# Side work of the key and value jobs reordered in a gated cross-attention kernel

## The reference

```python
h = layernorm(x)                        # x: 32 sequences of 64 tokens, 512 wide
q = rope(h @ wq)                        # 32 heads of 128
k, v = rope(ctx @ wk), ctx @ wv         # 8 key/value heads of 128
attn = softmax(q k^T / sqrt(128) + mask)
x = x + tanh(g_xattn) * ((attn v) @ wo)
h = layernorm(x)
logits = h @ route_w.T                  # 8 experts, top 1, weighted by its logit
x = x + tanh(g_ffn) * lora(h, A[e], B[e])   # rank 16
```

## Time and profile before

| | us |
|---|---|
| median of 3 runs | 1186.3 |
| lowest, highest | 1183.96, 1186.74 |
| the profiled execution: its own time | 1188.29 |
| its span, first to last instruction | 1186.3 |
| PE busy | 1128.3 (95%) |
| DVE busy | 921.5 (78%) |
| ACT busy | 632.5 (53%) |
| POOL busy | 567.9 (48%) |
| mean granted TensorE clock | 0.987 of full speed |

### The profile page before, as it was taken

How to read it: one execution, slowest core, us unless ns; L and a number is a source line. 1 busy time by engine, 2 the same in 40 slices (tenths; PEclk the granted TensorE clock), 3 DMA queues, 4 the chain that set the end, 5 groups by cost and what they waited for, 6 DMA issues and landing times.

```text
span 1186.3 us, 17218 instructions
## 1 busy us (share of the span) xinstructions
PE 1128.3 (95%) x5792; PEld 925.9 (78%) x5792; DVE 921.5 (78%) x1408; ACT 632.5 (53%) x1090; POOL 567.9 (48%) x517
## 2 busy tenths in 40 slices
PE   7899899779999999999999999999999999999997
PEld 6688788667777787777777777888888888888775
DVE  7773755768787888787888888888888888778886
ACT  6352345546666665656665544555555555555441
POOL 4650457866676666666663323233333333333320
PEclk9899899889999999999999999999999999999999
DMA  6869955374444444454448825542424353522201
GB/s 226 250 194 358 302 174 221 106 276 160 160 160 160 168 167 168 168 175 169 163 147 308 302 65 169 187 167 92 161 89 160 105 193 115 167 89 98 63 1 72
DMA packets 88902, 197.89 MB, mean 167 GB/s; under 512 B 8304, under 2 KB 41200, under 8 KB 82928
## 3 DMA queue, kind: packets, MB, share of 16 engines
q1 hardware_dynamic: 88816, 196.79, 48.6%
HBM read 113.92 MB, written 82.84 MB: 166 GB/s over the span
## 4 chain that ended last, share of the span: by engine, by line
PE 51%; POOL 14%; DVE 14%; issue 13%; ACT 4%; DMA 2%; SPq 1%; DVEq 0%; POOLq 0%; ACTq 0%
PE attn L845 18%; PE proj L783 13%; PE score L800 4%; POOL rot L1570 4%; PE attn L735 4%; PE turned L735 2%; DVE o_s L1117 2%; DVE q_r L1032 2%; POOL wq_s L1545 2%; DVE p_low L1110 2%; PE score L735 2%; PE turned L811 2%; DVE acc L1129 2%; PE attn L827 1%; ACT p_high L1391 1%
## 5 line engine op out<-in xcount | busy, mean ns | idle before, releaser
L845 PE MATMUL attn<-wo_s,o_s 128*128 128x512 f32 x1536 | 384.5, 399 | 15.9 <-DVE o_s L1117 15.9
L783 PE MATMUL proj<-xB,wq_s 128*128 128x512 f32 x1344 | 345.1, 400 | 7.8 <-DVE q_r L1074 5.1
L845 PEld LDWEIGHTS attn<-wo_s,o_s 128*128 128x128 f32 x1536 | 280.6, 188 | 87.2 <-DVE o_s L1117 31.4
L1570 POOL TENSOR_TENSOR rot<-rot,tab 128x512 f32<-128x512 f32 x160 | 216.8, 1356 | 224.5 <-ACT rot L1354 224.4
L783 PEld LDWEIGHTS proj<-xB,wq_s 128*128 128x128 f32 x1344 | 249.5, 190 | 69.1 <-DVE q_r L1074 5.9
L1037 DVE TENSOR_TENSOR q_r<-q_r,rot 128x512 f32<-128x512 f32 x128 | 124.8, 975 | 47.5 <-POOL rot L1570 36.6
L1399 ACT ACTIVATE o_s<-attn 128x512 fp32r<-128x512 f32 x128 | 69.6, 596 | 148.3 <-PE attn L831 148.1
L1032 DVE TENSOR_TENSOR q_r<-q_r,tab 128x512 f32<-128x512 f32 x128 | 140.7, 1099 | 3.1 <-ACT rot L1354 3.0
L1129 DVE SCALAR_TENSOR_TENSOR acc<-attn,gates_t,acc 128x512 f32<-128x512 f32 x128 | 96.0, 750 | 52.9 <-PE attn L845 50.9
L800 PEld LDWEIGHTS score<-k_r,q_r 128*128 128x128 f32 x1024 | 124.3, 192 | 7.3 <-issue 2.6
L800 PE MATMUL score<-k_r,q_r 128*128 128x64 f32 x1024 | 121.8, 272 | 0.2 <-DVE prob_even L1094 0.2
(11 more groups left out here) (174 smaller groups left out, 1485.2 us busy)
## 6 DMA issues: line engine op xcount, KB each, us to landing
wq_kept<-wq_s SPq DMA_DIRECT2D x16, 1792.0 KB, 6.6
wq_s<-wq_kept SPq DMA_DIRECT2D x16, 1792.0 KB, 8.7
v_kept<-vst SPq DMA_DIRECT2D x64, 256.0 KB, 4.1
v_s<-v_kept SPq DMA_DIRECT2D x128, 128.0 KB, 4.9
wo_kept<-wo_s SPq DMA_DIRECT2D x32, 512.0 KB, 2.9
wo_s<-wo_kept SPq DMA_DIRECT2D x32, 512.0 KB, 5.8
k_kept<-kst SPq DMA_DIRECT2D x32, 256.0 KB, 2.2
wq_raw<-in_wq SPq DMA_DIRECT2D x16, 512.0 KB, 7.7
```

What stands on the lines that cost most here:

```text
L783: last = e.matmul(dst[:, :], wq_s[:, b % 2, A, s, kt, :], xB[:, B, mv, kt, :], start=(first and kt == 0 and m == 0), stop=(kt == 1 and m = ...
L845: last = e.matmul(attn[bp][:, :], o_s[:, s, bp, h, :], wo_s[n % WO_SLOTS][:, m, :], start=(h == 0 and i == 0), stop=(h == GROUP - 1 and i ...
L1570: e.tensor_tensor(r3, r3, sin, ALU.mult).then_inc(times_sin, 1)
```

## The change

- `VST` goes from 3 to 4: four staging places for values.
- `X_BESIDE` moves each pair one or two jobs earlier (9, 12, 14, 17, 34, 37, 40, 43 become 8, 11, 13, 16, 32, 35, 38, 41), `X_TURN` goes from 3 to 4, and `combine_x` stands at the head of GpSimd's next job. The first pair of x is fetched one job earlier.
- The low halves of wv(2,1), wv(3,1), wo0, wo1 and wo2 move from GpSimd to VectorE. From job 56 on VectorE makes a weight's low half in the job itself and behind its `rope_add`.
- The store and the later fetch of each `xB` block have a semaphore of their own, so ScalarE waits for the blocks it overwrites next, not for all seven.
- On GpSimd the ropes' `by_sin` stand ahead of `combine_weights` and `weight_low` in each job. In step 0 the first rope and the low halves of (3, 0) and (3, 1) stand ahead of `combine_weights(3)`.
- VectorE masks the first scores ahead of finishing job 62, GpSimd subtracts their maximum at the head of job 62, and ScalarE takes the exponential at its end rather than behind job 63.
- ScalarE splits the pieces (3, 2) and (3, 3) in step 1 and no longer at the end of step 0.

```diff
-VST, KST = 3, 4
+VST, KST = 4, 4
...
-X_BESIDE = {9: 4, 12: 5, 14: 6, 17: 7, 34: 0, 37: 1, 40: 2, 43: 3}
-X_TURN, X_PLACES = 3, 3
+X_BESIDE = {8: 4, 11: 5, 13: 6, 16: 7, 32: 0, 35: 1, 38: 2, 41: 3}
+X_COMBINE, X_TURN, X_PLACES = 1, 4, 3
...
-X_FETCH = [7, 8, 9] + [n + X_TURN + 1 for n in list(X_BESIDE)[:-X_PLACES]]
+X_FETCH = [6, 8, 9] + [n + X_TURN + 1 for n in list(X_BESIDE)[:-X_PLACES]]
...
 def low_on_vector(w):
-    return w[0] in ("ctx", "wk") or (w[0] == "wo" and w[1] % GROUP == 3)
+    if w[0] == "wo":
+        return w[1] < GROUP or w[1] % GROUP == 3
+    return w[0] in ("ctx", "wk") or (w[0] == "wv" and w[2] == 1 and w[1] >= 2)
...
@@ vector, jobs
+                if n == SCORES_AFTER:
+                    mask_scores(0)
                 finish_job(n)
...
-                for w in SPLITS_BESIDE.get(n + 1, ()):
+                for w in SPLITS_BESIDE.get(n + 1, ()) if n + 1 < KEYS_3_MADE else ():
                     raw_low(w)
                 finish_key(JOBS[n])
+                for w in SPLITS_BESIDE.get(n, ()) if n >= KEYS_3_MADE else ():
+                    raw_low(w)
...
-                if n == SCORES_AFTER:
-                    mask_scores(0)
@@ scalar
-                    elif X_NO[pair] == CHUNK_TILES and i == 0:
-                        e.wait_ge(xB_stored, 16 * BLOCKS)
+                    elif X_NO[pair] == CHUNK_TILES:
+                        for B in range(BLOCKS)[2 * i:2 * i + 2]:
+                            e.wait_ge(xB_moved[B], 16)
...
+                if n == SCORES_AFTER:
+                    exponential(0)
...
-            exponential(0)
...
-                if k % 2 == 0:
+                if k % 2 == 0 or k == 1:
                     for w in weights_of(k):
                         wq_split(*w)
...
-                if k % 2 == 0:
+                if k % 2 == 0 and k:
                     for w in weights_of(k + 1):
                         wq_split(*w)
@@ gpsimd, jobs
-                for w in SPLITS_BESIDE.get(n, ()):
+                early = n < VALUES_MADE
+                if n == SCORES_AFTER:
+                    subtract_max(0)
+                for w in SPLITS_BESIDE.get(n, ()) if early else ():
                     raw_low(w)
+                if n - X_COMBINE in X_BESIDE:
+                    combine_x(X_BESIDE[n - X_COMBINE])
                 if n in X_BESIDE:
                     x_norms(X_BESIDE[n])
+                if JOBS[n][0] == "k":
+                    by_sin(ROPE_NO[JOBS[n]])
+                if n in ROPE_BESIDE:
+                    by_sin(ROPE_NO["q", *ROPE_BESIDE[n]])
                 if n in COMBINED_BESIDE:
                     combine_weights(COMBINED_BESIDE[n])
                 for w in WQ_BESIDE.get(n, ()):
                     weight_low(*w)
-                if JOBS[n][0] == "k":
-                    by_sin(ROPE_NO[JOBS[n]])
-                if n in ROPE_BESIDE:
-                    by_sin(ROPE_NO["q", *ROPE_BESIDE[n]])
-                if n in X_BESIDE:
-                    combine_x(X_BESIDE[n])
-                if n == SCORES_AFTER:
-                    subtract_max(0)
+                for w in SPLITS_BESIDE.get(n, ()) if not early else ():
+                    raw_low(w)
@@ gpsimd, step 0
+                    for q in ropes[0]:
+                        by_sin(ROPE_NO["q", *q])
+                    weight_low(*pieces[0])
+                    weight_low(*pieces[1])
+                    for q in ropes[1]:
+                        by_sin(ROPE_NO["q", *q])
+                    combine_weights(pieces[0][0])
+                    for q in ropes[2]:
+                        by_sin(ROPE_NO["q", *q])
```

More of the change, by code:

```diff
@@ L346, in build @@
         first_in = [sem(f"first_in{i}") for i in range(len(FIRST))]
-        xB_in = [sem(f"xB_in{i}") for i in range(BLOCKS)]
+        xB_moved = [sem(f"xB_moved{i}") for i in range(BLOCKS)]
         raw_in = [sem(f"raw_in{i}") for i in range(RAW)]
@@ L357, in build @@
         wo_stored = [sem(f"wo_stored{i}") for i in range(WO_SLOTS)]
-        xB_stored = sem("xB_stored")
         stored = [sem(f"stored{t}") for t in range(HALF_TILES)]
@@ L597, in store_xB @@
                 e.dma_start(xB_kept[B].rearrange("p h k n -> p (h k n)"),
-                            xB[:, B].rearrange("p h k n -> p (h k n)").bitcast(F32)).then_inc(xB_stored, 16)
+                            xB[:, B].rearrange("p h k n -> p (h k n)").bitcast(F32)).then_inc(xB_moved[B], 16)
             def fetch_xB(i):
@@ L602, in fetch_xB @@
                 e.wait_ge(produced, BLOCKS * (HEAD_PAIRS_ALL - 1) + i + 1)
-                if i == 0:
-                    e.wait_ge(xB_stored, 16 * BLOCKS)
+                e.wait_ge(xB_moved[B], 16)
                 e.dma_start(xB[:, B].rearrange("p h k n -> p (h k n)").bitcast(F32),
-                            xB_kept[B].rearrange("p h k n -> p (h k n)")).then_inc(xB_in[B], 16)
+                            xB_kept[B].rearrange("p h k n -> p (h k n)")).then_inc(xB_moved[B], 16)
             for w in FIRST[:BEFORE_JOBS]:
@@ L773, in product @@
                 if b == HEAD_PAIRS_ALL:
-                    e.wait_ge(xB_in[B], 16)
+                    e.wait_ge(xB_moved[B], 32)
                 if b < HEAD_PAIRS_ALL:
@@ L1610, in _ @@
                     subtract_max(k)
-                if pieces and k % 2 == 0:
-                    combine_weights(pieces[0][0])
[L1613 to L1624, removed]
+                    if pieces and k % 2 == 0:
+                        combine_weights(pieces[0][0])
+                    if pieces and k % 4 == 3:
+                        weight_low(*pieces[0])
+                    normalise(k)
+                    if pieces and k % 4 != 3:
+                        weight_low(*pieces[0])
+                    for q in ropes[0]:
+                        by_sin(ROPE_NO["q", *q])
+                    if pieces:
+                        weight_low(*pieces[1])
+                    for q in ropes[1] + ropes[2]:
+                        by_sin(ROPE_NO["q", *q])
+                else:
+                    for q in ropes[0]:
+                        by_sin(ROPE_NO["q", *q])
+                    weight_low(*pieces[0])
+                    weight_low(*pieces[1])
+                    for q in ropes[1]:
+                        by_sin(ROPE_NO["q", *q])
+                    combine_weights(pieces[0][0])
+                    for q in ropes[2]:
+                        by_sin(ROPE_NO["q", *q])
                 for n in wo_late(k):
```

## The result

The changed kernel takes 1173.15 us (median of 4 runs, 1171.59 to 1174.4) against 1185.38 us for the kernel before in the same session (1183.96 to 1186.74): a ratio of 0.9896, 95% interval 0.9878 to 0.9915, or 12.2 us less. Its profiled execution took 1174.4 us by its own time, 1172.3 of it span, against 1188.29 and 1186.3: 14.0 us less in the span. The forecast was 1170, or 16.4 us less.

A forecast was written before the change was run, and what follows sets the result against it. TensorE was taken to bound the kernel, with idle and half-clock time before 270 us to win back. Gains of 5.2 (A), 6.2 (B) and 5.0 (196 to 270 us) sum to 16.4: median 1170 us, range 1159 to 1180.

The forecast's parts named there:

- Hole A: TensorE's 4.8 us wait in job 12 for a low half of wv from GpSimd; gain 2.2 plus spell 3.0.
- The walk without turn-taking: Job 12: if VectorE and GpSimd don't alternate, wv(3,1) ends at 44.6 and the stall is 1.1 us; forecast took 2.6.
- the spell: TensorE's time at the lower clock (1.2 of 2.4 GHz) after a hole, priced at 3.0 us each.
- Hole B: TensorE's 3.2 us wait in the transposes after job 37 for GpSimd's sums of x; gain 3.2 plus spell 3.0.
- rival 4: Fourth staging place swallowed by full DMA queues and hole B stays: 1176 us, chance 0.08.
- Holes C and D: Waits ahead of product (1,3), 2.0 us for ScalarE's copy, and (1,6), 4.5 us for VectorE's sum; together give 1.0.
- Hole E: Waits of 1.1 us before first probability transposes, 4.6 before first values product; stage 196 to 270 us gives 5.0.
- the 32 us to be had: Most the change could give before 270 us: 20.2 us of holes and 12 of lower-clock spells.
- Later steps keep their order and their cost.: From 270 us to the end the span changes by no more than 2 us.
- Rival 1: GpSimd and VectorE hold each other up less; product (1,6) waits under 2 us: 1161 us, chance 0.2.
- rival 2: Stage of ropes gives nothing or job 12 keeps its spell: 1175 to 1178 us, chance 0.2.
- nor 3: Rival: moved blocks delay the rope chain on GpSimd between jobs 56 and 63: slower, 1194 us, chance 0.05.

The follow-up runs named there:

- e8: Changed kernel with three staging places for values (VST 3) as before, instead of four: 1174.15 us, ratio 0.9896.
- e2: Kernel before, with the changed kernel's order from job 48 on only: 1183.03 us, ratio 0.9967.
- e10: Changed kernel with 16 extra matmuls, whose result nobody reads, on TensorE before product (1,6): 1174.54 us, ratio 0.990.
- e4: Changed kernel run again unaltered, for a second profile: 1173.17 us (of three executions), ratio 0.9889.
- e11: Changed kernel run again unaltered, in a later session: 1174.43 us, ratio 0.9878.
- e3: Changed kernel with VectorE's query sums (1,1) and (1,2) in job 59 instead of job 60: 1173.9 us, ratio 0.9888.
- e7: Changed kernel with GpSimd's combine_weights(2) and four weight halves in its idle time, and sums (1,1), (1,2) in job 59: 1172.15 us, ratio 0.9884.
- e9: Changed kernel with GpSimd's three blocks and VectorE's low halves of wo1 and wo2 moved into idle time: 1171.8 us, ratio 0.9876.

## Why the prediction was right, and where it was not

**Hole A: 5.2 forecast, 5.1 measured, in part by luck.** The walk without turn-taking was the right one for VectorE. Its rows around the two halves of wv, and GpSimd's for the sums of x beside them:

```profile
41.71 0.69 DVE L1028 TENSOR_TENSOR ctxT<-near_raw,ctxT 128x512 fp32r<-128x512 f32 x1
42.31 0.68 DVE L1028 TENSOR_TENSOR wv_s<-near_raw,wv_s 128x512 fp32r<-128x512 f32 x1
42.92 0.68 DVE L1053 TENSOR_TENSOR vst<-turned,vst 128x512 fp32r<-128x512 f32 x1
43.52 0.68 DVE L1028 TENSOR_TENSOR ctxT<-near_raw,ctxT 128x512 fp32r<-128x512 f32 x1
44.12 0.68 DVE L1028 TENSOR_TENSOR wv_s<-near_raw,wv_s 128x512 fp32r<-128x512 f32 x1
44.72 0.68 DVE L1053 TENSOR_TENSOR vst<-attn,vst 128x512 fp32r<-128x512 f32 x1
```

```profile
41.88 1.72 POOL L1560 TENSOR_TENSOR combined<-raw 128x256 f32<-128x256 f32 x1 [0.96 <-DVE raw L1008]
43.55 1.84 POOL L1561 TENSOR_TENSOR combined<-raw 128x256 f32<-128x256 f32 x1
...
198.59 0.74 POOL L1540 TENSOR_TENSOR combined<-wq_raw 128x256 f32<-128x256 f32 x1
```

wv(3,1) was ready at 44.8 (44.12 + 0.68), and job 12 waited 0.8 us for it, not 2.6. VectorE, whose instructions followed each other without a gap, was not slowed; GpSimd's sums took 1.7 to 1.8 us, where one of the same shape took 0.74 elsewhere. They came late for their transposes, and TensorE waited 1.2 there, 2.0 in all. The two engines do hold each other up, but who pays was not known. The hole thus gave 2.8, not 2.2, and the spell 2.3, not 3.0; the two errors cancel. The Trainium skill (SBUF — State Buffer, section "Who interferes with whom") has it that the order of issue decides who blocks. These rows agree in part: each sum began just behind a half of VectorE (41.88 behind 41.71, 43.55 behind 43.52) and was held up. But the halves at 42.31 and 44.12 began after the sums and were not. Each sum ended with VectorE's next instruction that reads PSUM (42.92 + 0.68 = 43.60, and 45.4). No spell followed, as forecast.

**Hole B: 6.2 forecast, 6.3 measured.** 3.2 of hole and 3.1 for its spell. e8 shows that the fourth place, to which the prediction gave a share, has none that can be told: that half of rival 4 holds. e2 shows that the spell of before was not certain: with the hole at 2.98 us it did not come. That the profile of before had it is luck for the sum.

**Holes C and D: 1.0 forecast, 2.0 measured.** C went as said, and D stayed, on the engine and in the size said (4 to 6 us; it was 4.6, the walk had 5.9). The walk charged turns to nearly every rope_add, which was too much (of the five from 203 to 217 us two took 1.78, one 1.21 and two 0.7), and none to wo2's low half, put at 0.6, which took 1.75.

**Hole E: the stage from job 48, 5.0 forecast, 6.0 measured (17.2 - 11.2).** C and D alone give 1.0 more than forecast; behind them two errors of 0.7 cancel. The lead gained up to the values product was forecast at 3.5 and is 5.2 (16.4 - 11.2); what follows it, the spell less what is given back, was forecast at 1.5 and is 0.8 (17.2 - 16.4). The prediction had the spell go whole, as its hole fell to 1.4; the hole fell to 1.1, and half of the spell remained, 0.07 of 24 us for the 0.14 of the earlier trace rows.

**The price of a spell.** Three us each was right for B, too high for A (2.3) and wrong for D, whose spell the prediction kept at full price among the 32 us to be had. e10 shows nothing to be had there: behind D the chain of ropes binds, not TensorE.

**What failed: "Later steps keep their order and their cost."** By step 3 the lead was 17.2 against 16.4 forecast. Then 3.2 us went, 1.6 at the first expert and 1.6 at step 62, and the span from 270 us on changed by more than the 2 us that the prediction named as its limit. The waits of TensorE there are before's (2.41 and 2.37 us at the expert); what differs is the clock behind them. The step that failed is that steps with unchanged waits keep their cost. At the expert this is no effect of the change: e4 and e11, the same kernel, have that clock at 1.00 in one execution and lower in the other. At step 62 all three profiles of the changed kernel have the longer spell (6.8 us, where before has 3.4), and whether the change brings it stays open. Why a wait of one length draws a spell in one execution and not in the next is open too. Rival 1 did not come (product (1,6) waits 4.6 us), nor rival 2 (the stage gave 6.0, and A kept no spell), nor 3, nor 4 (B went).

For the profiled execution the sum gave 1171.9 us and it took 1174.4: 3.2 lost later, 0.8 more won before (with rounding, 2.5). The median of 1173.15 is 3 above the forecast of 1170, since the forecast took it 2.0 below the profiled execution and it lies 1.25 below. As a gain in the medians, 12.2 us came of the 16.4.

## What to carry to other kernels

Find the in-order list that ends last and walk it: moving one consumer along it (e3, e7) moves the hole, while putting a side block into that engine's measured idle time (e9) shortens it. Charge for time at the lower clock only where TensorE's own work is the next thing late, and nothing where another engine's chain ends later (e10). Take the lead at the same instruction group in both traces at several places, and repeat the profile before a loss of one or two us in an untouched stretch is blamed on the change, or cleared of it (e4, e11).

## What the runs showed of the hardware

- The lower clock after a short wait of TensorE is no function of the wait's length: the 2.4 us at the first expert were followed by it in seven profiles (at 1.4 to 1.7 us of the lead) and not in the other seven, before's among them. Hole B was followed by it in before (3.2 us) and not in e2 (2.98 us). Behind hole A, 4.84 us in both, it lasted 6.8 us in before and 3.4 in e2.
- VectorE's subtraction of 128x512 with both inputs in SBUF took 0.68 us at job 12, while GpSimd's sums stretched from 0.74 to 1.72 and 1.84, and 1.75 at hole D, where GpSimd's multiply had begun first (212.54) and ended at 214.09, 0.55 before it. The rows of VectorE and GpSimd:

```profile
212.89 1.75 DVE L1028 TENSOR_TENSOR wo_s<-raw,wo_s 128x512 fp32r<-128x512 f32 x1
```

```profile
212.54 1.55 POOL L1575 TENSOR_TENSOR rot<-rot,tab 128x512 f32<-128x512 f32 x1 [0.29 <-ACT rot L1358]
```

- Low-clock time can cost nothing: 16 added matmuls brought the clock from 0.79 to 1.00 over 16 us, and the first transposes came 18.0 us after product (1,6) with and without them.
